# Small-head attention on one core: the preparation of the last three local batches over 24 slots in place of 16, with two preparations under way at once

## Chip, core and metric

The kernel runs on one core of a Trainium2 chip. The metric is the device time of one execution in microseconds (us), the median of several. Before the change it is 2004.02 us (three runs, 2002.38 to 2004.36).

## What is computed

The program is a chain of eight residual stages on a stream of 4 x 512 tokens of width 128, all in float32: gated linear attention, a two-layer windowed-attention block, the small-head attention of this case, the windowed block again, attention over heads, experts, full attention, experts. The stage that the change touches computes, with 16 query heads and 4 key heads of 8 elements each:

```
def global_latent_attn(x, wq, w_kv_down, w_k_up, w_v_up, wo):
    q = split_heads(x @ wq, H)
    latent = x @ w_kv_down
    k = split_heads(latent @ w_k_up, KVH)
    v = split_heads(latent @ w_v_up, KVH)
    ...
def local_gqa_attn(x, wq, wk, wv, wo):
    q = split_heads(x @ wq, H)
    k = split_heads(x @ wk, KVH)
    v = split_heads(x @ wv, KVH)
    q, k = (rope(q, BASE_L), rope(k, BASE_L))
    q, k = (qk_norm(q), qk_norm(k))
    k, v = (repeat_kv(k), repeat_kv(v))
    mask = (diff >= 0) & (diff < WIN)
    return merge_heads(sdpa(q, k, v, mask)) @ wo
```

WIN is 32. The input of the stage is a layer norm of the stream; the global attention's result is added to it, an RMS norm follows, then the local attention, and both are added to the stream.

## The kernel before

Every engine has a queue of its own that is written out by hand; between engines there are semaphores. The work of this stage is `small_heads`, one function of that name for each of TensorE (PE, L629), ScalarE (ACT, L1174), VectorE (DVE, L1701) and GpSimd (POOL, L2151).

A **batch** k is one of the 4 sequences in one of the 2 attentions: 0 to 3 are global, 4 to 7 local. A batch has four **units** U = 4k to 4k+3 (one query head of each of the four key groups), and a unit four **slots** j = 0 to 3 (key tiles of 128). In each slot PE computes transposed scores for four heads (`scores`, L678, into two PSUM pairs used in turn), ACT takes their exponential (L1210), a mask is multiplied in, by POOL for even slots (L2188) and by DVE for odd ones (L1770), and one unit later PE multiplies by the values (`values`, L691). For local batches a slot has 160 queries, for global ones up to 512. Two units later `finish` drains the sums: DVE copies them out of PSUM in slot 0 (L1777), PE transposes them back in slot 1 (L328, a helper that all transposes share), DVE divides (L1785, L1786). In the second unit of the next batch, PE transposes the heads in slot 2, ACT copies (L973, a helper), PE applies the output weights in slot 3 (L710) and DVE adds (L1794).

Beside the units of batch k runs the **preparation** of batch k+1, in 16 steps i; step i stood in slot i of the batch's 16. For a local batch:

- step 0: PE transposes the normalised stream (bank 4); DVE sums its squares (L1721 to L1725)
- step 1: ACT copies it, scaled, to `xT` (L1185)
- step 4: PE projects q into bank 4 (L652), k and v into bank 5 (L659)
- step 5: DVE copies q and k out and squares them (L1728 to L1730); step 6: sums (L1734, L1736)
- step 7: ACT takes Ln, then Exp (L1192, L1193), each with a table load ahead of it
- step 8: DVE scales q, k and v (L1742, L1743); step 9: two rotary products (L1750, L1751)
- step 10: POOL adds them (L2167); step 11: DVE makes four copies of k (L1756)
- step 12: PE transposes q and k into banks 4 and 5 (L328); step 13: ACT copies q (L973), DVE writes k four times (L1761)

Within a slot, DVE does `finish`, then the mask of an odd slot, then the preparation's step; PE does scores, `finish`, the step, values. The two lines that set this on PE are the same on the other engines but for the bound:

```
if U < 28:
    prepare(U // NR + 1, NR * (U % NR) + j)
```

The first scores of a batch wait for step 13 of its preparation on ACT and DVE (`b_qT_in`, `b_kT_in`). q and k are kept in two buffers (k % 2); the PSUM banks 4 and 5, `b_rs`, `b_ms`, `b_sq` and `xT` are single.

Of the kernel before, what the change touches and what calls it, by code (L numbers as in the profile page):

```python
# [15 lines left out]
ALU = mybir.AluOpType  # L16
# [8 lines left out]
NB = 4  # L25
S = 512
NT = S // P
# [84 lines left out]
def program(nc, x_in, w_in, c_in, r_in, out, scratch, c_at):  # L112
# [3 lines left out]
    with ExitStack() as ctx:  # L116
# [206 lines left out]
        def _(pe):  # L323
# [305 lines left out]
            def small_heads():  # L629
                unit = lambda U: (U // NR, U % NR, U < 16)  # L630

                def prepare(k, i):
                    glob = k < NB
                    if i == 0:
                        if glob:
                            pe.wait_ge(gs.ln, 2 * NB + k + 1)
                        else:
                            pe.wait_ge(s.b_add, k - NB + 1)
                        need(pe, s.b_qT_in, k)
                        transposes(4, lambda j: Y[:, NT * (k % NB) + j, :]).then_inc(s.b_xT_ps, 1)  # L640
                    elif i == 2 and glob:
                        pe.wait_ge(s.b_hT, k + 1)
                        need(pe, s.b_kT_in, k)
                        mm(ps[0:32, 5, :], W("b_down"), xT[:, :], start=True, stop=True).then_inc(s.b_lat_ps, 1)
                    elif i == 4:
                        pe.wait_ge(s.b_hT, k + 1)
                        need(pe, s.b_kT_in, k)
                        if glob:
                            pe.wait_ge(s.b_lat_in, k + 1)
                        for j in range(NT):  # L650
                            t = slice(j * P, (j + 1) * P)
                            mm(ps[:, 4, t], xT[:, t], W("b_gq" if glob else "b_lq"), start=True, stop=True)  # L652
                        for j in range(NT):
                            t = slice(j * P, (j + 1) * P)
                            o = ps[:, 5, 64 * j:64 * j + 64]
                            if glob:
                                last = mm(o, b_latT[0:32, t], W("b_up")[0:32, :], start=True, stop=True)
                            else:
                                last = mm(o, xT[:, t], W("b_lkv"), start=True, stop=True)  # L659
                        last.then_inc(s.b_kvq, 1)  # L660
                    elif i == 12:
                        pe.wait_ge(s.b_rope, k + 1)
                        pe.wait_ge(s.b_qn, k + 1)
                        transposes(4, lambda j: b_qr[:, j, 0:HB, :].rearrange("p h d -> p (h d)"))
                        pe.wait_ge(s.b_kr, k + 1)
                        transposes(5, lambda j: b_kr[:, j].rearrange("p g r d -> p (g r d)")).then_inc(s.b_tps, 1)

                def scores(U, j, gp):
                    k, r, glob = unit(U)
                    st = 8 * U + 2 * j + gp  # L670
                    if r == 0 and j == 0 and gp == 0:
                        pe.wait_ge(s.b_qT_in, k + 1)
                        pe.wait_ge(s.b_kT_in, k + 1)
                    need(pe, s.b_exp, st - 1)
                    n = small_width(glob, j)
                    for hh in range(2):
                        rows = slice(64 * gp + 32 * hh, 64 * gp + 32 * hh + 32)
                        last = mm(ps[:, 2 * (st % 2) + hh, 0:n], b_kT[rows, k % 2, r, j * P:(j + 1) * P],  # L678
                                  b_qT[rows, k % 2, j * P:j * P + n], start=True, stop=True)
                    last.then_inc(s.b_s, 1)  # L680

                def values(U, j):
                    k, r, glob = unit(U)
                    if j == 0:
                        need(pe, s.b_div, U - 1)
                        need(pe, s.b_add, k if U % 2 else 0)
                    pe.wait_ge(s.b_mask_v if j % 2 else s.b_mask_p, 2 * U + j // 2 + 1)
                    n, at = small_width(glob, j), small_at(glob, j)
                    for g in range(NG):
                        rows = slice(32 * g, 32 * g + 32)  # L690
                        last = mm(ps[rows, 6 + U % 2, j * P:j * P + n], b_vx[:, k % 2, j, g, :],  # L691
                                  b_p[:, U % 2, g, at:at + n], start=j == 0, stop=True, skip_group_check=True)
                    if j == NT - 1:
                        last.then_inc(s.b_pv, 1)

                def finish(U, j):
                    V = U - 2
                    if j == 1 and 0 <= V < 32:
                        pe.wait_ge(s.b_o_in, V + 1)
                        transposes(6 + V % 2, lambda i: b_oR[:, V % NR, i * P:(i + 1) * P]).then_inc(s.b_rT, 1)  # L700
                    k = (U - 5) // NR
                    if U % NR == 1 and 0 <= k < 2 * NB:
                        if j == 2:
                            pe.wait_ge(s.b_div, NR * k + 4)
                            transposes(7, lambda i: b_os[:, i].rearrange("p g r d -> p (g r d)"))\
                                .then_inc(s.b_oT_ps, 1)
                        elif j == 3:
                            pe.wait_ge(s.b_oT_in, k + 1)
                            for i in range(NT):
                                last = mm(ps[:, 7, i * P:(i + 1) * P], b_oT[:, i * P:(i + 1) * P],  # L710
                                          W("b_gwo" if k < NB else "b_lwo"), start=True, stop=True)
                            last.then_inc(s.b_out, 1)

                pe.wait_ge(s.b_zero, 1)
                for i in range(16):
                    prepare(0, i)
                for U in range(34):
                    for j in range(NT):
                        if U < 32:
                            scores(U, j, 0)  # L720
                            scores(U, j, 1)
                        finish(U, j)
                        if U < 28:
                            prepare(U // NR + 1, NR * (U % NR) + j)
                        if 1 <= U <= 32:
                            values(U - 1, j)

# [242 lines left out]
        def _(act):  # L970
# [203 lines left out]
            def small_heads():  # L1174
# [23 lines left out]
                for i in range(16):  # L1198
                    prepare(0, i)
                for U in range(34):  # L1200
                    k, glob = U // NR, U < 16
                    for j in range(NT):
                        if U < 32:
                            for gp in range(2):
                                st = 8 * U + 2 * j + gp
                                act.wait_ge(s.b_s, st + 1)
                                if j == 0 and gp == 0:
                                    need(act, s.b_pv, U - 1)
                                n, at, b = small_width(glob, j), small_at(glob, j), 2 * (st % 2)
                                act.activation(b_p[:, U % 2, 2 * gp:2 * gp + 2, at:at + n], ps[:, b:b + 2, 0:n],  # L1210
                                               ACT.Exp, scale=float(HD) ** -0.5).then_inc(s.b_exp, 1)
                        finish(U, j)
                        if U < 28:
                            prepare(k + 1, NR * (U % NR) + j)

            def head_attention():

# [192 lines left out]
        def _(dve):  # L1410
# [290 lines left out]
            def small_heads():  # L1701
# [99 lines left out]
                for U in range(34):  # L1801
                    for j in range(NT):
                        finish(U, j)
                        if U < 32 and j % 2:
                            mask(U, j)
                        if U < 28:
                            prepare(U // NR + 1, NR * (U % NR) + j)
                        if j == 2 and U in (2, 6):
                            fresh(U // 4 + 2)
                dve.wait_ge(s.b_add, 2 * NB)  # L1810
# [290 lines left out]
        def _(pool):  # L2101
# [49 lines left out]
            def small_heads():  # L2151
# [8 lines left out]
                        .then_inc(gs.root4, 1)  # L2160

                def prepare(k, i):
                    if i == 10 and k < 2 * NB:
                        pool.wait_ge(s.b_rt, k + 1)
                        need(pool, s.b_tps, k)
                        pairs = lambda a: a.rearrange("p j h (n b) -> p (j h n) b", b=2)
                        pool.tensor_tensor(pairs(b_qr), pairs(b_t[0]), pairs(b_t[1])[:, :, ::-1], ALU.add)\  # L2167
                            .then_inc(s.b_rope, 1)
                    elif i == 2 and k > NB:
                        z = k - NB - 1  # L2170
                        pool.wait_ge(s.b_add, z + 1)
                        x = X[:, NT * z:NT * z + NT, :]
                        pool.tensor_tensor(x, x, Y[:, NT * z:NT * z + NT, :], ALU.add).then_inc(s.b_xy, 1)

                root4()
                for i in range(16):
# [3 lines left out]
                for U in range(34):  # L2180
                    glob = U < 16
                    for j in range(NT):
                        if U < 32 and j % 2 == 0:
# [3 lines left out]
                            m = C("causal" if glob else "local", 0, n)  # L2187
                            pool.tensor_tensor(v, v, m.unsqueeze(1).broadcast_to([P, NG, n]), ALU.mult)\  # L2188
                                .then_inc(s.b_mask_p, 1)
                        if U < 32:  # L2190
                            prepare(U // NR + 1, NR * (U % NR) + j)
                        if j == 2 and U in (2, 6):
                            root4()

# [297 lines left out]
    return sum(small_width(glob, i) for i in range(j))  # L2492


def rows_at(n):

    return 0 <= n < TT
# [68 lines left out]
```

## Time and profile before

| | |
|---|---|
| runs | 2002.38, 2004.02, 2004.36 us |
| profiled execution | 2001.43 us; span of its instructions 1999.6 us |
| PE busy | 1628.7 us (81%) |
| DVE busy | 1240.1 us (62%) |
| ACT busy | 1074.5 us (54%) |
| POOL busy | 907.4 us (45%) |
| mean granted TensorE clock | 0.908 |

A time in the trace counts from the span's start. A busy time is the sum over an engine's instructions; in a timeline each row gives the start, how long it took, the engine and line, and in brackets how long the engine had stood idle before it and what released it ("issue": nothing that the profile shows). The granted clock is 1.00 at 2.4 GHz and 0.50 at 1.2 GHz. The local batches run from 953.92 us (U = 16) on.

### The profile page before, as it was taken

What the parts mean: (1) busy time and instruction counts of PE and PEld (TensorE: products, weight loads), DVE (VectorE), ACT (ScalarE), POOL (GpSimd) and SP (SyncE); (2) the same over time, 40 slices, a digit from 0 to 9 for tenths busy, and PEclk for the clock granted to TensorE, in tenths of its full rate; (3) what the DMA queues carried; (4) which work ended last, traced back from release to release, by engine and by line L of the source; (5) the groups of instructions that cost most, each with busy time, mean ns of one, the idle gap of its engine ahead of it and who ended that gap; (6) DMA issues with size and microseconds to landing.
All of it is one profiled execution on the core that took longest, in us unless ns stands there. A gap on an engine that the chain in (4) does not pass through costs nothing. (4 is left out here: it accounts for less than half of the span.)

```text
span 1999.6 us, 37978 instructions
## 1 busy us (share of the span) xinstructions
PE 1628.7 (81%) x13323; PEld 1163.0 (58%) x13323; DVE 1240.1 (62%) x3746; ACT 1074.5 (54%) x2751; POOL 907.4 (45%) x668
## 2 busy tenths in 40 slices
PE   6999996899989965888878788999976675958877
PEld 5888884566666643334544465666654453646655
DVE  4555554787777733555674687777754985736565
ACT  3555553678787732566453577777762112323432
POOL 2333333766556511223443666566622664432034
PEclk9999998999999985899876799999998896978989
DMA  4000000111111100000000011111100001110012
GB/s 200 1 1 1 1 1 9 27 27 25 30 27 25 25 6 1 1 1 1 1 1 1 19 29 31 26 26 25 25 20 1 0 0 28 26 32 1 1 43 22
DMA packets 41082, 38.64 MB, mean 19 GB/s; under 512 B 21944, under 2 KB 32192, under 8 KB 40512
## 3 DMA queue, kind: packets, MB, share of 16 engines
q1 hardware_dynamic: 35264, 32.02, 6.1%
q0 software_dynamic: 5632, 4.20, 1.7%
q8 instruction: 110, 1.80, 0.4%
q14 instruction: 76, 0.62, 0.1%
HBM read 13.14 MB, written 4.20 MB: 9 GB/s over the span
## 5 line engine op out<-in xcount | busy, mean ns | idle before, releaser
L973 ACT ACTIVATE arena<-ps 128x512 f32<-128x512 f32 (+4 forms) x670 | 356.4, 587 | 267.2 <-PE ps L328 101.9
L1210 ACT ACTIVATE arena<-ps 128x320 f32<-128x320 f32 (+4 forms) x256 | 132.6, 561 | 137.3 <-PE ps L678 134.4
L1110 ACT ACTIVATE arena<-arena,g_small 128x128 f32<-128x128 f32 x512 | 199.0, 404 | 0.5
L1606 DVE CUSTOM_DVE_ANT_0 arena<-ps,consts,g_ss 128x128 f32<-128x128 f32 x512 | 145.5, 346 | 79.8 <-PE ps L484 78.1
L2188 POOL TENSOR_TENSOR arena<-arena,consts 128x512 f32<-128x512 f32 (+1 forms) x64 | 93.7, 1464 | 195.6 <-ACT arena L1210 195.6
L328 PE MATMUL ps<-consts,arena 128*128 128x128 f32 x400 | 82.2, 344 | 108.2 <-DVE arena L1466 47.3
L2209 POOL TENSOR_TENSOR arena<-arena 128x512 f32<-128x512 f32 x64 | 82.1, 1283 | 186.5 <-DVE arena L1614 186.4
L678 PE MATMUL ps<-arena 32*128 32x160 f32 (+4 forms) x1024 | 122.3, 468 | 20.7 <-ACT arena L1210 10.2
L328 PEld LDWEIGHTS ps<-consts,arena 128*128 128x128 f32 x400 | 56.3, 173 | 139.1 <-DVE arena L1466 52.3
L1613 DVE TENSOR_TENSOR arena<-ps,tabs 128x512 f32<-128x512 f32 x128 | 87.5, 684 | 51.7 <-ACT arena L1079 45.0
L678 PEld LDWEIGHTS ps<-arena 32*128 32x128 f32 x1024 | 61.9, 213 | 88.1 <-ACT arena L1210 54.1
L1550 DVE TENSOR_REDUCE arena<-arena 128x8 f32<-128x1032 f32 x32 | 39.3, 1228 | 117.9 <-ACT arena L1030 117.9
L2219 POOL TENSOR_TENSOR g_ss<-g_ss,consts 128x8 f32<-128x8 f32 x64 | 105.5, 1648 | 7.0
L2136 POOL TENSOR_TENSOR arena<-arena,consts 128x8 f32<-128x8 f32 x32 | 52.8, 1649 | 122.2 <-PE ps L420 96.5
L585 PE MATMUL ps<-arena,weights 128*128 128x512 f32 (+1 forms) x192 | 101.6, 640 | 5.9 <-ACT arena L1139 3.9
L2259 POOL TENSOR_TENSOR arena<-arena 128x2048 f32<-128x2048 f32 x16 | 86.8, 5434 | 42.7 <-ACT arena L1232 42.7
L2222 POOL TENSOR_TENSOR g_ss<-g_ss,consts 128x8 f32<-128x8 f32 x64 | 104.8, 1638 | 0.0
L1110 ACT ACTIVATION_READ_ACCUMULATOR arena<-arena,g_small 128x1 f32 x512 | 103.8, 203 | 0.0
L2017 DVE SCALAR_TENSOR_TENSOR arena<-ps,arena 128x128 f32<-128x128 f32 x256 | 72.0, 343 | 43.8 <-PE ps L904 29.9
L2212 POOL TENSOR_TENSOR arena<-arena 128x512 f32<-128x512 f32 x64 | 81.4, 1272 | 39.0 <-issue 35.2
L742 PE MATMUL ps<-arena,consts 128*128 128x256 f32 x256 | 70.2, 435 | 34.6 <-DVE arena L1819 34.6
L691 PE MATMUL ps<-arena 128*32 128x160 f32 (+4 forms) x1024 | 87.5, 415 | 5.0 <-issue 5.0
(256 smaller groups left out, 4171.3 us busy)
## 6 DMA issues: line engine op xcount, KB each, us to landing
arena<-arena SPq DMA_DIRECT2D x112, 128.0 KB, 2.3
weights<-in_w SPq DMA_DIRECT2D x1, 5069.0 KB, 24.4
weights<-in_w SPq DMA_DIRECT2D x1, 2052.0 KB, 12.8
arena<-Y SPq DMA_DIRECT2D x64, 32.0 KB
arena<-Y SPq DMA_DIRECT2D x64, 31.8 KB
consts<-in_c SPq DMA_DIRECT2D x1, 1278.0 KB, 9.0
sorted_rows<-X SPq DMA_DIRECT2D x1, 1024.0 KB, 5.1
X<-sorted_rows SPq DMA_DIRECT2D x4, 256.0 KB, 3.7
```

The lines of the kernel that those rows point to most:

```text
L328: last = tr(ps[:, bank, j * P:(j + 1) * P], src(j), ident)
L585: mm(ps[0:m, 4 + c % 2, :], W("f_w1", at, at + m), g_hnT, start=True, stop=True)\
L678: last = mm(ps[:, 2 * (st % 2) + hh, 0:n], b_kT[rows, k % 2, r, j * P:(j + 1) * P], b_qT[rows, k % 2, j * P:j * P + n], start=True, stop=True)
L691: last = mm(ps[rows, 6 + U % 2, j * P:j * P + n], b_vx[:, k % 2, j, g, :], b_p[:, U % 2, g, at:at + n], start=j == 0, stop=True, skip_grou ...
L973: copy = lambda o, i: act.activation(o, i, ACT.Copy)
L1110: last = act.activation(g_p[:, n % 2, 4 * hf + i, :], g_sc[:, 4 * hf + i, :], ACT.Exp, scale=-1.0, bias=g_mn[:, h:h + 1], accum_out=g_rs[: ...
L1210: act.activation(b_p[:, U % 2, 2 * gp:2 * gp + 2, at:at + n], ps[:, b:b + 2, 0:n], ACT.Exp, scale=float(HD) ** -0.5).then_inc(s.b_exp, 1)
L1606: last = dve.tensor_tensor_reduce(g_sc[:, 4 * hf + i, :], ps[:, 4 + hf, i * P:(i + 1) * P], C("mask_f" if n % NT else "mask_f0"), g_ss[:, ...
L1613: tt(heads(low[0]), heads(src), table(tabs_at), ALU.mult)
L2188: pool.tensor_tensor(v, v, m.unsqueeze(1).broadcast_to([P, NG, n]), ALU.mult)\
L2219: stepped_after(pool.tensor_tensor(ss[:, 8:16], ss[:, 8:16], C("neghalf", 0, 8), ALU.pow))
L2222: pool.tensor_tensor(ss[:, 0:8], ss[:, 0:8], C("neghalf", 0, 8), ALU.pow).then_inc(gs.root, 1)
```

## The change

The preparations of batches 5, 6 and 7 (`EARLY`) are laid over 24 slots, from eight slots before the batch that they run beside. Step i stands at the offset `EARLY_SLOTS[i] - 8`: steps 0 to 3 at -8 to -5, step 4 at -1, steps 5, 6, 7 at 0, 1, 2, steps 8, 9, 10 at 4, 5, 6, step 11 at 8, step 12 at 10, step 13 at 11. Preparations 0 to 4 stay. Three waits on PE go with it. The adding of the two streams on POOL gets a function of its own and keeps its place.

```
@@ PE, prepare
-                        need(pe, s.b_qT_in, k)
+                        need(pe, s.b_ss if k in EARLY else s.b_qT_in, k)
                         transposes(4, lambda j: Y[:, NT * (k % NB) + j, :]).then_inc(s.b_xT_ps, 1)
...
                     elif i == 4:
                         pe.wait_ge(s.b_hT, k + 1)
+                        need(pe, s.b_qT_in, k)
                         need(pe, s.b_kT_in, k)
...
                     elif i == 12:
                         pe.wait_ge(s.b_rope, k + 1)
                         pe.wait_ge(s.b_qn, k + 1)
+                        if k + 1 in EARLY:
+                            pe.wait_ge(s.b_hT, k + 2)
@@ PE, ACT, DVE alike
-                        if U < 28:
-                            prepare(U // NR + 1, NR * (U % NR) + j)
+                        for k, i in prepared_at(NR * U + j):
+                            prepare(k, i)
@@ POOL
-                    if i == 10 and k < 2 * NB:
+                    if i == 10:
...
-                    elif i == 2 and k > NB:
-                        z = k - NB - 1
-                        pool.wait_ge(s.b_add, z + 1)
-                        x = X[:, NT * z:NT * z + NT, :]
-                        pool.tensor_tensor(x, x, Y[:, NT * z:NT * z + NT, :], ALU.add).then_inc(s.b_xy, 1)
+                def add_streams(z):
+                    pool.wait_ge(s.b_add, z + 1)
+                    x = X[:, NT * z:NT * z + NT, :]
+                    pool.tensor_tensor(x, x, Y[:, NT * z:NT * z + NT, :], ALU.add).then_inc(s.b_xy, 1)
...
-                        if U < 32:
-                            prepare(U // NR + 1, NR * (U % NR) + j)
+                        for k, i in prepared_at(NR * U + j):
+                            prepare(k, i)
+                        if j == 2 and U in (16, 20, 24, 28):
+                            add_streams((U - 16) // NR)
@@ new
+EARLY = (5, 6, 7)
+EARLY_SLOTS = (0, 1, 2, 3, 7, 8, 9, 10, 12, 13, 14, 16, 18, 19, 20, 21)
+
+def prepared_at(slot):
+
+    return [(k, i) for k in range(1, 2 * NB) for i in range(16)
+            if slot == 16 * (k - 1) + (EARLY_SLOTS[i] - 8 if k in EARLY else i)]
```

In the changed kernel the lines of DVE and ACT stand 3 further down (L1761 is L1764, L1777 is L1780, L1770 is L1773, L1756 is L1759, L1721 is L1724, L1210 is L1213, L1192 is L1195).

**DVE, third unit of a local batch (U = 18, with the preparation of batch 5), up to the copy of the fourth.** Before:

```order
L1777 COPY arena<-ps 128x512
L1742 TENSOR_TENSOR arena<-arena,b_rs 128x640
L1743 TENSOR_TENSOR arena<-ps,b_rs 128x16x8
L1785 RECIPROCAL b_ri<-ps 128x16
L1786 TENSOR_TENSOR arena<-ps,b_ri 128x16x8
L1770 TENSOR_TENSOR arena<-arena,consts 128x4x160
L1750 TENSOR_TENSOR arena<-arena,consts 128x640
L1751 TENSOR_TENSOR arena<-arena,consts 128x640
L1770 TENSOR_TENSOR arena<-arena,consts 128x4x128
L1756 COPY arena<-arena 128x16x8 x4
L1777 COPY arena<-ps 128x512
```

and of the change, from the same L1777 (now L1780) to that of the unit after:

```order
L1780 COPY arena<-ps 128x512
L1759 COPY arena<-arena 128x16x8 x4
L1724 TENSOR_TENSOR arena<-Y 128x4x128
L1726 TENSOR_REDUCE b_rs<-arena 128x4
L1727 TENSOR_SCALAR b_rs<-b_rs 128x4
L1728 TENSOR_SCALAR b_ms<-b_rs 128x4
L1788 RECIPROCAL b_ri<-ps 128x16
L1789 TENSOR_TENSOR arena<-ps,b_ri 128x16x8
L1773 TENSOR_TENSOR arena<-arena,consts 128x4x160
L1773 TENSOR_TENSOR arena<-arena,consts 128x4x128
L1764 TENSOR_SCALAR arena<-ps,consts 128x512 x4
L1780 COPY arena<-ps 128x512
```

Steps 8 and 9 have left the third unit, and steps 11 and 13 of this preparation and step 0 of the next have come in; step 13 (L1764) now stands between the unit's last mask and the copy of the next unit.

**ACT, the exponentials around step 7 (preparation of batch 7).** Before, after the exponentials of a second unit's last slot (128 queries):

```order
L1210 ACTIVATE arena<-ps 128x2x160 x6
L973 ACTIVATE arena<-ps 128x512
L1210 ACTIVATE arena<-ps 128x2x128 x2
L1192 ACT_TABLE_LOAD
L1192 ACTIVATE b_rs<-b_rs 128x84
L1193 ACT_TABLE_LOAD
L1193 ACTIVATE b_rs<-b_rs 128x84
L1210 ACTIVATE arena<-ps 128x2x160 x6
```

and of the change, before the exponentials of the first unit's last slot:

```order
L1213 ACTIVATE arena<-ps 128x2x160 x6
L1195 ACT_TABLE_LOAD
L1195 ACTIVATE b_rs<-b_rs 128x84
L1196 ACT_TABLE_LOAD
L1196 ACTIVATE b_rs<-b_rs 128x84
L1213 ACTIVATE arena<-ps 128x2x128 x2
L1213 ACTIVATE arena<-ps 128x2x160 x6
```

The two table loads are as many as before; they have moved from between the second and third unit into the first.

## Rows read from the trace of the kernel before

**Rows 1.** The page: its first line.

```profile
span 1999.6 us, 37978 instructions
```

**Rows 2.** Stretches: length, busy time (instructions) by engine, granted clock, DMA share, GB/s.

```profile
953.92:990.52 36.60, 30.48 (x312) 17.53 (x313) 24.64 (x43) 16.48 (x39) 16.27 (x10) 0.77 0.01 1
990.52:1024.65 34.13, 27.88 (x313) 17.14 (x313) 24.84 (x43) 16.48 (x39) 16.61 (x10) 0.80 0.01 1
...
1060.00:1076.90 16.90, 16.90 (x141) 10.04 (x140) 5.29 (x11) 5.95 (x16) 7.80 (x5) 0.50 0.00 1
1077.00:1086.00 9.00, 8.66 (x118) 5.23 (x120) 4.78 (x9) 5.30 (x14) 4.75 (x4) 1.00 0.01 3
```

**Rows 3.** Timeline of PE, third and fourth unit beside preparation 6, and next start.

```profile
1005.63 0.48 PE L691 MATMUL ps<-arena 128*32 128x160 f32 x8 [1.57 <-issue]
1007.20 0.87 PE L678 MATMUL ps<-arena 32*128 32x160 f32 x8 [1.09 <-ACT arena L1210]
...
1014.87 1.11 PE L328 MATMUL ps<-consts,arena 128*128 128x128 f32 x4 [1.75 <-POOL arena L2167]
1016.86 1.11 PE L328 MATMUL ps<-consts,arena 128*128 128x128 f32 x4 [0.87 <-DVE arena L1756]
...
1024.65 0.55 PE L678 MATMUL ps<-arena 32*128 32x160 f32 x8 [0.85 <-DVE arena L1761]
```

**Rows 4.** Timeline of PE: start of unit 16, and step 4 of preparation 6.

```profile
953.92 0.70 PE L678 MATMUL ps<-arena 32*128 32x160 f32 x8 [0.98 <-issue]
...
996.33 1.16 PE L652 MATMUL ps<-weights,xT 128*128 128x128 f32 x8
997.33 1.00 PE L659 MATMUL ps<-weights,xT 128*128 128x64 f32 x8
```

**Rows 5.** Timeline of PE: starts of units 25, 28, 29, 30, and output weights.

```profile
1029.79 0.74 PE L678 MATMUL ps<-arena 32*128 32x160 f32 x8
...
1058.75 0.55 PE L678 MATMUL ps<-arena 32*128 32x160 f32 x8 [0.85 <-DVE arena L1761]
...
1065.79 0.92 PE L678 MATMUL ps<-arena 32*128 32x160 f32 x8
...
1073.46 2.08 PE L710 MATMUL ps<-weights,arena 128*128 128x128 f32 x8
...
1076.05 0.92 PE L678 MATMUL ps<-arena 32*128 32x160 f32 x8
```

**Rows 6.** Timeline of DVE: steps 5 to 6, 11, 13, a mask, L1777, step 0.

```profile
1001.08 0.68 DVE L1728 COPY arena<-ps 128x512 f32<-128x512 f32 x1
...
1004.69 0.24 DVE L1736 SCALAR_TENSOR_TENSOR b_rs<-b_rs,b_ms 128x80 f32<-128x80 f32 x1
...
1014.85 1.95 DVE L1756 COPY arena<-arena 128x128 f32<-128x128 f32 x4 [1.43 <-POOL arena L2167]
...
1021.83 2.72 DVE L1761 TENSOR_SCALAR arena<-ps,consts 128x512 f32<-128x512 f32 x4
1024.47 0.68 DVE L1770 TENSOR_TENSOR arena<-arena,consts 128x512 f32<-128x512 f32 x1
1025.07 0.68 DVE L1777 COPY arena<-ps 128x512 f32<-128x512 f32 x1
1025.67 0.68 DVE L1721 TENSOR_TENSOR arena<-Y 128x512 f32<-128x512 f32 x1
...
1028.02 0.26 DVE L1785 RECIPROCAL b_ri<-ps 128x16 f32<-128x16 f32 x1
...
1028.52 0.81 DVE L1770 TENSOR_TENSOR arena<-arena,consts 128x640 f32<-128x640 f32 x1
```

**Rows 7.** Timeline of ACT: step 7 of preparation 6, and the exponentials behind it.

```profile
1002.84 1.28 ACT L1192 ACT_TABLE_LOAD   x1
1004.97 0.27 ACT L1192 ACTIVATE b_rs<-b_rs 128x84 f32<-128x84 f32 x1 [0.84 <-DVE b_rs L1736]
...
1006.73 0.75 ACT L1210 ACTIVATE arena<-ps 128x320 f32<-128x320 f32 x2
```

More of the change, by code:

```diff
@@ L1200, in small_heads @@
                 for U in range(34):
-                    k, glob = U // NR, U < 16
+                    glob = U < 16
                     for j in range(NT):
@@ L1212, in small_heads @@
                         finish(U, j)
-                        if U < 28:
-                            prepare(k + 1, NR * (U % NR) + j)
+                        for k, i in prepared_at(NR * U + j):
+                            prepare(k, i)
             def head_attention():
@@ L1805, in small_heads @@
                             mask(U, j)
-                        if U < 28:
-                            prepare(U // NR + 1, NR * (U % NR) + j)
+                        for k, i in prepared_at(NR * U + j):
+                            prepare(k, i)
                         if j == 2 and U in (2, 6):
@@ L2189, in small_heads @@
                                 .then_inc(s.b_mask_p, 1)
-                        if U < 32:
-                            prepare(U // NR + 1, NR * (U % NR) + j)
+                        for k, i in prepared_at(NR * U + j):
+                            prepare(k, i)
+                        if j == 2 and U in (16, 20, 24, 28):
+                            add_streams((U - 16) // NR)
                         if j == 2 and U in (2, 6):
```

## The prediction, made before the changed kernel had run

> **What bounds the kernel now.** The execution's span is 1999.6 us [rows 1]; I first cut out the stage that changes by batches. The local batches beside which a preparation runs take 36.60 us and 34.13 us [rows 2], the third 34.10 us (from 1024.65 [rows 3] to 1058.75 [rows 5]); the last, with no preparation beside it, is some 27 us to its last values. In the 34.13 us no engine is full: PE is busy 27.9, DVE 24.8, ACT 16.5, POOL 16.6 [rows 2]. So no engine's sum is the bound but the order in which they wait for each other, and I went on to PE's timeline.
>
> There PE stands idle five times per batch [rows 3]: 1.57 us and 1.09 us as the third unit starts, 1.75 us and 0.87 us at step 12, 0.85 us before the next batch's first scores. The first is put down to nothing, but `values` waits there for `b_add`, and DVE comes to L1794 only behind steps 5 and 6. The second is ACT's, behind the table loads of step 7 [rows 7]. The third and fourth are step 12 waiting for steps 10 and 11, the fifth is step 13 (L1761, 2.65 us from its start to the next mask [rows 6]). In all 6.13 us. The granted clock is the other half: 0.80 over the batch. A unit at full clock takes 5.14 us with step 0 in it (1024.65 [rows 3] to 1029.79 [rows 5]), one at half clock 7.04 us without a step (1058.75 to 1065.79), and 10.26 us with the output weights in it (1065.79 to 1076.05, L710 alone 2.08) [rows 5].
>
> **The change part by part.** No instruction is added or taken away; I walk a batch of the changed kernel unit by unit, t from each unit's start, from these rows.
>
> *Waits that go.* Step 5 and 6 are no longer ahead of L1794 (1.57 us). Between steps 10, 11 and 12 there are now two slots each: POOL's add is done a unit before L1756 wants it, and L1756 before PE wants it (1.75 and 0.87 us). Step 13 ends a unit before the next batch (0.85 us). What is late next is below. POOL's queue gets step 10 ahead of another mask, nothing else; the adding of the streams stays; SP has nothing in this stage.
>
> *First unit.* DVE does L1777 (0.6), steps 5 and 6 (3.85, from 1001.08 to the end of L1736 at 1004.93), between them a division (0.5) and a mask (0.6 to 0.75) [rows 6]: it ends at 5.75 us, or up to 6.45 us where POOL's masks slow it. ACT has then loaded its table and waits, as it does now for 0.84 us; from Ln to the next exponentials is 1.76 us (1004.97 to 1006.73) [rows 7], from there to PE's next scores 0.47 (1007.20 [rows 3]). So the second unit starts at 8.0 to 8.7 us; I take 8.4, nearer the crowded end since POOL masks twice there. PE has work for about 4.5 us of it (5.14 less step 0): it idles nearly 4 us at a stretch. The table loads cost more than the 2.66 us of today, since DVE's steps 5 and 6 start only with the unit.
>
> *Second unit.* After 1.57 and 1.09 us of idling PE fell to half clock today (the L678 behind it takes 0.87 in place of 0.55 [rows 3]); after 4 us it will too. The unit is then unit 29 again: 10.26 us at half clock throughout, some 9.6 with the first slots still at full; I take 10.0. Steps 8, 9 on DVE and 10 on POOL lie beside it.
>
> *Third unit.* In unit 29 the clock came back behind L710 (1.00 from 1077 us on [rows 2]). So full clock: 5.14 with step 0, and step 12, 8 transposes, which took 1.1 for four at half clock [rows 3] and so some 1.3 for eight at full: 6.7 with its queueing. DVE does L1777, L1756 (up to 1.95 beside a POOL mask), step 0 and a division (2.85, from 1025.67 to 1028.52), a mask [rows 6]: some 6.2 us, beside PE. The added wait of step 12 for `b_hT` is for ACT's copy one slot before, done by then: nothing; uncovered it would be one copy of 512 columns, some 0.6 as DVE's [rows 6]. Behind it on PE stand values and all scores. Step 0's wait on `b_ss` was met nearly a unit earlier.
>
> *Fourth unit.* Here is the new wait. DVE's queue reads: mask of the third unit's last slot, step 13, then L1777, and PE's transposes in slot 1 wait for that copy. The mask can start at 0.2 us, when the exponentials are done; 0.6 + 2.65 + 0.6 [rows 6] puts the copy's end at 4.1 us. PE is there after one slot and one pair of scores, at 1.4. It idles 2.7 us. Behind it are two and a half slots and step 4: 3.2 (5.14 less step 0 and the 1.4) and 2.0 [rows 4], so 5.3 at full clock; at half 4.7 and 4.1, so 8.8. PE fell to half clock after 0.85 us of idling before unit 28 [rows 5], so it will here; step 4's dense matmuls should bring it back. I take 7.6, the unit 11.7.
>
> A batch: 8.4 + 10.0 + 6.7 + 11.7 = 36.8 us, for the batches of units 16 to 19 and 20 to 23. Beside units 24 to 27 there are no steps 0 and 4: third unit 6.2 (step 12 waits for L1756), fourth 4.1 and between 3.2 and 4.7, I take 4.5: 8.4 + 10.0 + 6.2 + 8.6 = 33.2.
>
> *Ahead of it.* Step 0 of preparation 5 moves into global unit 14, where it lies in a wait that ACT sets; step 4 into the last slot of unit 15. There it waits for `b_kT_in`, as unit 16's scores do for 0.98 us [rows 4], and so that wait is not made longer but by 0.35, and its own 2.0 us come on top: 2.4 us. It would be 0 only if PE had that long to wait there, which it has not.
>
> **The sum.** 2.4 + 2 x 36.8 + 33.2 = 109.2 us against 36.60 + 34.13 + 34.10 = 104.8: 4.4 us longer. The last batch keeps its 27 us: it was at half clock from just after its start [rows 5] and will be. The profiled execution ran 2001.43 us, so 2005.8 for it; the median of the runs stands 2.6 higher, so 2008.4. A measurement of this kernel can tell about 0.2%, 4 us, from no change.
>
> Bounds: with the fourth unit's rest at full clock it is 2.3 x 2 + 1.3 less (minus 1.5 in all), and with the first unit 0.4 and the second 0.4 shorter, three times, minus 3.9; with rest, first and second unit at their upper ends, plus 8.7.
>
> **A rule against the trace.** From 1060 to 1076.9 us PE was busy for 16.90 of 16.90 us and stayed at 0.50 all the time [rows 2]. The Trainium skill ("TensorE: Matmul & The Clock Gate", Part 1, What's actually happening) holds that "the default state is throttled, and activity releases the throttle", by how busy PE has been. By that rule alone a gapless second unit would soon be back at full clock; this trace does not agree for a stretch of 32-row scores and values, and only with L710 did the clock rise. The rival that follows is the first below.
>
> **The rivals.**
> *The clock comes back early in the second unit.* The unit then takes 5.14 less step 0's 0.6 plus 0.6 for the head transposes and 1.1 for L710 at half its 2.08, wait by wait 6.9 in all with its queueing. DVE becomes the bound after it: L1794 and mask 1.2, L1777 0.6, L1756 1.95, step 0 and division 2.85, two masks 1.35, step 13 2.65, L1777 0.6 make 11.2 from the third unit's start to PE's transposes in the fourth. A batch is 8.4 + 6.9 + 11.2 + 5.3 = 31.8, the third 28.8 (mask and step 13 behind its exponentials): 2.4 + 63.6 + 28.8 = 94.8, 10 us shorter than before; with the fourth unit's rest at half clock 4 shorter. I put 7 shorter, 1997. For it: the second unit has two sets of dense transposes and L710. Against: unit 29 had the same and came up only at its end. It decides from a rise before the middle of the unit.
> *The clock holds in the fourth unit* although PE idles 2.7 us: 1.5 us shorter than before, 2002.5. For it: at units 20 and 24 the 0.85 us cost no clock, dense transposes being near (unit 24 to 25 is full clock [rows 3, 5]). Against: the gap is three times as long.
> *The clock never rises* in the third unit: 7.04 + 1.1 + 2.2 = 10.4 for it, the fourth 1.3 of waiting, 7.04 and 4.1 = 12.4, batch 42: 15 to 20 us slower, 2021. For it: today the batches' 0.80 means 40% of 34 us, 14 us, at half clock [rows 2], well past one unit; against: L710.
> *The copy is not waited for*, because PE comes later than I reckon. Then the fourth unit saves 2.7 us; that needs a third unit over 9 us, which is no gain either, so it has no number of its own.
>
> **How the numbers follow.** My forecast, half clock in most of the fourth unit: 0.54, of which 0.34 is over 4 us slower and 0.20 within. The clock holds: 0.18 (0.15 within, 0.03 faster). It comes back early: 0.20, all faster. It never rises: 0.08, slower. Faster 0.23, same 0.35, slower 0.42. The range: 1998 takes in the lower bound and a third of the early clock, 2015 the upper bound; outside lie some 0.12 below and 0.07 above.
>
> **What would show it.** In the changed profile: no idle time of L328 released by POOL's add or by the copies of step 11; no wait at `values` for L1794; in each first unit a PE gap near 4 us up to the exponentials of its last slot; in each fourth unit one near 2.7 us before the transposes, released by the copy L1780; half clock through the second unit and into the fourth. Wrong if the fourth unit's gap is below 1 us, or if the second unit takes 7 us.

## The result and the profile after

| | before | changed |
|---|---|---|
| median (18 runs each, taken together) | 1999.56 us | 2007.71 us |
| lowest to highest | 1996.84 to 2007.59 | 2004.62 to 2013.47 |
| profiled execution: span | 1999.6 us [rows 1] | 2008.7 us |
| mean granted clock | 0.908 | 0.903 |

The changed kernel takes 1.004 times as long, 95% interval 1.003 to 1.0049: 8 us slower. The first three runs of before had a median of 2004.02 us; over 18 it is 1999.56, so the forecast of 2008.4 was 4.4 us of loss on a base that was 4.5 us high. That it lies so near 2007.71 is luck: a loss that was too small and a base that was too high.

The page of the changed kernel:

```profile
span 2008.7 us, 37984 instructions
PE 1637.3 (82%) x13323; PEld 1170.4 (58%) x13323; DVE 1237.7 (62%) x3746; ACT 1073.2 (53%) x2751; POOL 906.1 (45%) x668
```

The matmuls are the same in number (13323), as are those of DVE, ACT and POOL; PE's busy time is 8.6 us longer at a mean granted clock of 0.903 in place of 0.908. The stage cut by batches, as in [rows 2] (length, busy by engine, granted clock, DMA, GB/s); the rows begin at the first scores of units 16, 20, 24 and 28, the last is the tail at full clock:

```profile
957.47:997.37 39.90, 31.77 (x317) 19.02 (x313) 25.86 (x42) 16.38 (x39) 16.22 (x10) 0.76 0.00 1
997.37:1036.30 38.93, 34.11 (x317) 21.40 (x313) 23.03 (x42) 16.37 (x39) 16.22 (x10) 0.63 0.01 1
1036.30:1069.48 33.18, 28.68 (x296) 16.64 (x293) 19.75 (x38) 15.80 (x38) 16.18 (x10) 0.65 0.00 1
1069.48:1085.50 16.02, 16.02 (x152) 9.25 (x148) 5.60 (x11) 6.51 (x17) 8.04 (x6) 0.57 0.00 1
1085.50:1096.00 10.50, 10.16 (x148) 6.18 (x144) 6.06 (x12) 6.02 (x16) 5.64 (x4) 1.00 0.01 2
```

Unit 16 starts 3.55 us later (957.47, 953.92 in [rows 4]); then 39.90 against 36.60, 38.93 against 34.13, 33.18 against 34.10 us; and the last batch up to unit 31 gives back 1.6. That is +3.6 (unit 15 grew by 4.0 and 0.5 came off ahead of unit 14), +3.3, +4.8, -0.9, -1.6: 9.1 us, all of the spans' difference. In the second batch the clock is 0.63 where it was 0.80.

PE's timeline of that second batch, where [rows 3] had five gaps:

```profile
997.37 0.92 PE L681 MATMUL ps<-arena 32*128 32x160 f32 x8
...
1006.92 1.18 PE L681 MATMUL ps<-arena 32*128 32x160 f32 x8 [2.06 <-ACT arena L1213]
...
1014.63 2.08 PE L713 MATMUL ps<-weights,arena 128*128 128x128 f32 x8
...
1017.22 0.92 PE L681 MATMUL ps<-arena 32*128 32x160 f32 x8
...
1023.71 0.82 PE L681 MATMUL ps<-arena 32*128 32x160 f32 x8
...
1028.29 0.71 PE L328 MATMUL ps<-consts,arena 128*128 128x128 f32 x4 [2.61 <-DVE arena L1780]
...
1032.11 2.08 PE L653 MATMUL ps<-weights,xT 128*128 128x128 f32 x8
1033.98 1.81 PE L660 MATMUL ps<-weights,xT 128*128 128x64 f32 x8
1036.30 0.92 PE L681 MATMUL ps<-arena 32*128 32x160 f32 x8
```

The rows of L681 are the starts of units 20 to 24: 9.55, 10.30, 6.49 and 12.59 us. All five old gaps are gone; two new ones stand where the forecast put them, before the second unit's first scores (3.04 us in the first batch, 2.06 in the other two) and before the fourth unit's transposes. Step 4 runs at half clock (2.08 and 1.81 us; 1.16 and 1.00 in [rows 4]). DVE's timeline shows why the second gap is there; it answers to [rows 6]:

```profile
1022.79 2.20 DVE L1773 TENSOR_TENSOR arena<-arena,consts 128x640 f32<-128x640 f32 x2
1024.92 2.71 DVE L1764 TENSOR_SCALAR arena<-ps,consts 128x512 f32<-128x512 f32 x4
1027.55 0.68 DVE L1780 COPY arena<-ps 128x512 f32<-128x512 f32 x1
```

Two masks, step 13, then the copy that PE wants, 4.5 us after the fourth unit's start at 1023.71. In unit 19 the same gap is 4.85 us, in unit 27 2.27 us. What makes unit 19's so long is the last mask ahead of step 13, on DVE, which starts beside a mask of POOL:

```profile
983.62 2.03 DVE L1773 TENSOR_TENSOR arena<-arena,consts 128x512 f32<-128x512 f32 x1
```

```profile
983.57 1.53 POOL L2191 TENSOR_TENSOR arena<-arena,consts 128x640 f32<-128x640 f32 x1 [1.45 <-ACT arena L1213]
```

It takes 2.03 us there and 0.69 in unit 27, where it stands alone.

### The profile page after: what moved, and what is told of

Its sections match the earlier page's. It is cut to its first block and busy times, and to the rows that moved or that the text cites. A ratio compares the mean times of both kernels' runs of the same rounds, so it can differ in the third digit from the quotient of the medians.

```text
span 2008.7 us, 37984 instructions
## 1 busy us (share of the span) xinstructions
PE 1637.3 (82%) x13323; PEld 1170.4 (58%) x13323; DVE 1237.7 (62%) x3746; ACT 1073.2 (53%) x2751; POOL 906.1 (45%) x668
## 5 line engine op out<-in xcount | busy, mean ns | idle before, releaser
L1213 ACT ACTIVATE arena<-ps 128x320 f32<-128x320 f32 (+4 forms) x256 | 132.1, 561 | 148.5 <-PE ps L681 145.6
L681 PE MATMUL ps<-arena 32*128 32x160 f32 (+4 forms) x1024 | 125.9, 484 | 20.9 <-ACT arena L1213 13.8
L681 PEld LDWEIGHTS ps<-arena 32*128 32x128 f32 x1024 | 64.3, 223 | 90.5 <-ACT arena L1213 59.8
L907 PEld LDWEIGHTS ps<-weights,arena 128*128 128x128 f32 x512 | 69.4, 198 | 38.7 <-issue 36.8
```

Source lines behind the costliest of these rows:

```text
L907: last = mm(ps[:, 6 + q % 2, j * P:(j + 1) * P], e_h[:, q % 2, j * P:(j + 1) * P], W("e_w2", 128 * e, 128 * e + 128), start=True, stop=True)
```

## The experiments

Lengths of units come from PE's timeline in each run's profile, as above. Ratios are to the kernel before, run on the same chip.

### Step 13 two slots later

```
-                    elif i == 13:
+                    elif i == (15 if k in EARLY else 13):
                         dve.wait_ge(s.b_tps, k + 1)
```

> The changed kernel with one move: DVE's part of step 13 (four writes of k) stands two slots later, in slot 1 of the fourth unit behind its mask, in place of slot 3 of the third. Theory A (the copy of the fourth unit stands in the queue behind step 13, and PE waits for the copy): the gaps of 4.85, 2.61 and 2.27 us before the fourth units' transposes shrink to under 1 us, units 19, 23 and 27 (15.25, 12.59, 9.06 us) take about 8, 8 and 6.5, and the kernel is 12 to 14 us faster than the changed one, so 4 to 6 us faster than the one before. Theory B (DVE is simply full in the third unit, whatever the order): the gap stays over 2 us, or comes back as a wait of step 4 for the keys, and the time stays within 3 us of the changed kernel's, 5 to 8 us above the one before.

Measured: 2001.28 us, ratio 1.0008 (0.9993 to 1.0023); about 6 us faster than the changed kernel, level with before, and half of theory A's 12 to 14. The gaps before the fourth units' transposes are 2.22 and 0.66 us, and none in the third batch, from 4.85, 2.61 and 2.27; units 19, 23, 27 take 12.92, 10.74 and 6.64 us. So the order of the queue alone is worth 6 us. Theory B holds for the rest: step 4 on PE, and at the end the scores of unit 28, now wait for the keys.

```profile
1023.83 0.66 PE L328 MATMUL ps<-consts,arena 128*128 128x128 f32 x4 [0.66 <-DVE arena L1780]
...
1028.62 1.20 PE L653 MATMUL ps<-weights,xT 128*128 128x128 f32 x8 [1.90 <-DVE arena L1764]
```

### PE's gap filled with matmuls

```
                         if 1 <= U <= 32:
                             values(U - 1, j)
+                        if U in (16, 20, 24) and j == 3:
+                            pe.wait_ge(s.b_div, U - 1)
+                            for _ in range(12):
+                                tr(ps[:, 6, 384:512], ident, ident)
```

> The kernel of step13_late, with 12 transposes of a constant matrix added on PE behind the values of the last slot in units 16, 20 and 24, where PE waits for the table loads (their results are never read). Theory A (the second unit is slow because PE idles ahead of it and falls to half clock): with the gap filled the second units run at full clock, 7 us in place of 9 to 10, and the kernel is 4 to 8 us faster than step13_late. Theory B (the second unit takes what its waits on ACT and DVE make it, the clock hardly counts): its length stays within 1 us and the kernel within 2 us of step13_late.

Measured: 2000.77 us, ratio 1.0005 (0.9993 to 1.0017); not to be told from step13_late, so theory A's 4 to 8 us did not come. But the profile shows both halves of the rival that I had priced. Units 20 and 21 (first scores of the second unit at 1003.55, of the third at 1009.78), in PE's timeline and, below it, as stretches with the clock in the last but two columns:

```profile
1001.11 2.51 PE L733 MATMUL ps<-consts 128*128 128x128 f32 x12
1003.55 0.55 PE L681 MATMUL ps<-arena 32*128 32x160 f32 x8
...
1013.26 1.02 PE L328 MATMUL ps<-consts,arena 128*128 128x128 f32 x4 [1.17 <-DVE arena L1784]
```

```profile
1003.55:1009.78 6.23, 6.12 (x81) 3.97 (x80) 5.89 (x9) 3.44 (x9) 3.83 (x2) 1.00 0.01 3
1009.78:1018.65 8.87, 7.39 (x84) 4.55 (x80) 8.70 (x15) 3.31 (x9) 5.04 (x3) 0.81 0.00 0
```

With the gap filled the second unit ran at 1.00 and took 6.23 us, against 10.31 in step13_late (7.40 against 8.76, 6.23 against 10.31 in the other two batches). The third unit took 8.87 against 6.38, with DVE busy 8.70 of the 8.87 us. Over the three batches 9.5 us were won in the second units and 6.7 lost in the third: clock gained ahead of a full DVE is given back at DVE. The rest went in units 28 to 30, 22.50 us in place of 19.92, at a granted clock of 0.62 in place of 0.74.

### The table loads left out, in both kernels

```
-                        after(act.activation(b_rs[:, :], b_rs[:, :], ACT.Ln))
-                        act.activation(b_rs[:, :], b_rs[:, :], ACT.Exp, scale=-0.5).then_inc(s.b_rn, 1)
+                        fn = (ACT.Ln, ACT.Exp, -0.5) if k <= NB else (ACT.Copy, ACT.Copy, 0.003)
+                        after(act.activation(b_rs[:, :], b_rs[:, :], fn[0]))
+                        act.activation(b_rs[:, :], b_rs[:, :], fn[1], scale=fn[2]).then_inc(s.b_rn, 1)
```

> The changed kernel, where ACT applies two copies with a scale in place of Ln and Exp in step 7 of the preparations 5 to 7: left out are the reciprocal roots, so q, k and v have other sizes, and with them the two table loads of each. Theory A (the changed kernel's first unit ends with the table loads): units 16, 20, 24 (9.98, 9.55, 9.55 us) lose 2 to 3 us each, 7 to 9 us in all and a few more where the clock then stays up; 8 to 12 us faster than the changed kernel. Theory B (DVE's steps 5 and 6 set the end of the first unit): ACT then waits for them, and less than 3 us is gained.

> The kernel before with the same left out (the reciprocal roots of preparations 5 to 7, and the two table loads of each). Theory A (there PE's wait for b_add behind steps 5 and 6 on DVE covers more than half of the loads): 1.1 us less at each start of the third unit, 3 to 5 us in all with the clock. Theory B (the loads cost the same in both): 8 to 12 us.

Measured, changed kernel: 2001.55 us, ratio 1.0009 (0.9994 to 1.0024), some 6 us faster than with the loads. Units 16, 20, 24 take 8.67, 7.44 and 7.42 us, 1.3 to 2.1 less each, 5.6 in all: less than the 7 to 9 of theory A and more than theory B's 3. (The batch in which DVE's last mask meets POOL's changed too: the gap of the fourth unit is 2.61 us in the first batch and 4.93 in the second.) Kernel before: 1999.85 us, ratio 1.0 (0.9989 to 1.0012), nothing. There the third unit's gap of 1.09 us went and the fourth unit's grew from 1.75 [rows 3] to 4.26:

```profile
1013.06 1.12 PE L328 MATMUL ps<-consts,arena 128*128 128x128 f32 x4 [4.26 <-POOL arena L2168]
```

Step 12 waits there for POOL's add, and that for DVE's steps 8 and 9. On DVE, the stretch ahead of it:

```profile
1004.75 1.85 DVE L1743 TENSOR_TENSOR arena<-arena,b_rs 128x640 f32<-128x640 f32 x1
...
1007.33 2.21 DVE L1771 TENSOR_TENSOR arena<-arena,consts 128x640 f32<-128x640 f32 x1
```

Each of the two stands beside one of POOL's masks (1004.37 and 1007.31, 1.55 us each) and takes 1.0 and 1.4 us longer than the 0.82 of such an operation alone. Counted from the first scores of unit 20, step 8 starts 16.13 us in, where it started 16.34 us in with the loads, for DVE's own queue comes to it no sooner; step 11 stands at 24.41 in place of 24.33. So the loads were no bound of the kernel before: they were covered by DVE's queue and the chain DVE, POOL, DVE behind it. Whether something would have been gained had the two operations not met POOL's masks, this run does not show.

### DVE's part of step 13 on ACT, in both kernels

```
                         copy(b_qT[:, k % 2], ps[:, 4, :]).then_inc(s.b_qT_in, 1)
+                    if k > NB and i >= 13:
+                        for r in ((0,), (1, 2), (3,))[i - 13]:
+                            ins = act.activation(b_kT[:, k % 2, r, :], ps[:, 5, :], ACT.Copy, scale=C("rows", r, r + 1))
+                        if i == 15:
+                            ins.then_inc(s.b_kT_in, 1)
...
-                    elif i == 13:
+                    elif i == 13 and k <= NB:
                         dve.wait_ge(s.b_tps, k + 1)
```

> The changed kernel with DVE's part of step 13 (2.65 us a batch) given to ACT for the preparations 5 to 7: four scaled copies out of PSUM, one, two and one in the slots of steps 13, 14 and 15. Theory A (in the third unit DVE's queue is the bound, and filling PE's gap gained nothing for that reason): the fourth units' gaps before the transposes go under 0.5 us without the wait of step 4 that moving step 13 brought; 9 to 14 us faster than the changed kernel, 1 to 6 us faster than the one before. Theory B (the length of a batch is set by the chain through POOL and ACT): ACT's four copies delay the exponentials by as much, and it is no faster than step13_late, 2 us above the one before.

> The kernel before with the same edit. Theory A: only the 0.85 us before each batch's first scores goes, and some of PE's waits for the copies of step 12 stay (1.75 and 0.87 us): 2 to 3 us faster in all. Theory B (any work taken from DVE shortens the batch by as much): 6 to 8 us faster.

Measured, on the changed kernel: 1985.4 us, ratio 0.9943 (0.9925 to 0.9962): 0.6% faster than before (11 us by the ratio, 14 by the medians) and some 20 us faster than the changed kernel, well over theory A's 9 to 14. Its batches:

```profile
956.45:989.08 32.63, 28.66 (x317) 16.84 (x313) 22.22 (x38) 18.63 (x43) 16.22 (x10) 0.85 0.01 1
989.08:1020.40 31.32, 26.36 (x317) 16.67 (x313) 22.74 (x38) 18.63 (x43) 16.34 (x10) 0.89 0.01 2
1020.40:1049.51 29.11, 24.14 (x296) 14.81 (x292) 19.11 (x33) 17.73 (x42) 15.70 (x10) 0.88 0.01 1
```

and the fourth unit of the second, PE first, then ACT's last three writes between the exponentials:

```profile
1015.29 0.66 PE L328 MATMUL ps<-consts,arena 128*128 128x128 f32 x4 [0.38 <-DVE arena L1785]
...
1018.11 1.16 PE L653 MATMUL ps<-weights,xT 128*128 128x128 f32 x8
```

```profile
1013.53 0.79 ACT L1218 ACTIVATE arena<-ps 128x320 f32<-128x320 f32 x2
1014.16 1.31 ACT L1202 ACTIVATE arena<-ps,consts 128x512 f32<-128x512 f32 x2
1015.30 0.82 ACT L1218 ACTIVATE arena<-ps 128x320 f32<-128x320 f32 x2
1015.94 0.77 ACT L1202 ACTIVATE arena<-ps,consts 128x512 f32<-128x512 f32 x1
```

The gap is 0.38 us, step 4 waits for nothing and runs at full clock; the fourth units take 7.94, 8.03 and 5.81 us, from 15.25, 12.59 and 9.06. More than DVE's 2.65 us per batch was won since the gap was also what lowered the clock: 0.89 in the second batch, 0.63 before the edit. It shows behind the preparations too. Units 28 to 30, which have no preparation beside them and were not edited, as stretches with the columns of [rows 2], first in the kernel before, then here:

```profile
1058.75:1081.46 22.71, 22.43 (x216) 13.28 (x216) 8.23 (x16) 9.48 (x25) 10.09 (x7) 0.62 0.01 1
```

```profile
1049.51:1066.09 16.58, 16.19 (x221) 10.11 (x217) 9.90 (x16) 9.47 (x26) 10.98 (x8) 1.00 0.01 2
```

The same work takes 6.1 us less at 1.00 than at 0.62 (21.09 us at 0.67 in the changed kernel), and so these three units hold more than a third of the 15.7 us by which the two spans differ.

On the kernel before the same edit lost: 2006.54 us, ratio 1.0035 (1.0022 to 1.0047), where both theories had a gain. The last write stands one slot ahead of the next batch's first scores, and ACT makes it only after the exponentials of that slot's neighbours:

```profile
1024.88 0.92 PE L678 MATMUL ps<-arena 32*128 32x160 f32 x8 [0.94 <-ACT arena L1199]
1025.72 1.12 PE L328 MATMUL ps<-consts,Y 128*128 128x128 f32 x4
```

The wait is 0.94 us (1.48 in the first batch) for 0.85, and units 20 and 24 run partly at half clock, 6.59 and 7.14 us for 5.14; the third units after them take 9.67 and 9.68 for 8.70 and 8.68. In unit 20 the clock fell behind the wait. In unit 24 it had not come back ahead of it: it stood at 0.50 from unit 23's first scores through the wait, where in the kernel before it rose in unit 23's last slots (0.90 from 1021.9 us on). Why it does not rise there here, the runs do not settle.

### Preparation 5 back in its place

```
-EARLY = (5, 6, 7)
+EARLY = (6, 7)
```

> The changed kernel with preparation 5 back in its 16 slots; 6 and 7 stay spread. Theory A (my sum: ahead of unit 16 the change costs 2.4 us, the trace shows 4.0, and unit 16 is 2.4 us longer): units 15 and 16 are back at 18.3 from 24.7 us, and the kernel is 5 to 7 us faster than the changed one, 1 to 3 us slower than before. Theory B (those 6 us come back as waits in units 17 to 19, since preparation 5 has then to be made beside them): within 2 us of the changed kernel.

Measured: 2011.01 us, ratio 1.0064 (1.0047 to 1.008), 3 us slower than the changed kernel by the medians and 5 by the ratios, whose intervals just touch; not the gain of theory A. Units 15 and 16 are back at 10.69 and 7.63 us, as theory A had it, but unit 19 takes 19.67 us:

```profile
982.16 1.12 PE L328 MATMUL ps<-consts,arena 128*128 128x128 f32 x4 [4.95 <-POOL arena L2170]
```

Step 0 of preparation 6 now stands on DVE right behind step 8 of preparation 5 (973.22 to 977.3 us, L1724 to L1728), ahead of step 9, and POOL and PE wait for step 9. So theory B had the place of the loss right: the 6 us of units 15 and 16 are no pure loss of the change, and here they come back beside units 16 to 19 with more on top.

### An early start without the spreading

```
-            if slot == 16 * (k - 1) + (EARLY_SLOTS[i] - 8 if k in EARLY else i)]
+            if slot == 16 * (k - 1) + (i - {5: 2, 6: 4, 7: 4}.get(k, 0))]
```

with step 0's wait on `b_qT_in` as before and without the wait of step 12 on `b_hT`.

> The kernel before with preparation 5 started two slots earlier and 6 and 7 four, each in 16 consecutive slots: an early start without the spreading and without two in banks 4 and 5 at once. Theory A (PE's waits come from steps of one preparation in neighbouring slots): L328's 1.75 and 0.87 us stay, the 1.57 us at values goes since L1794 no longer stands behind steps 5 and 6, and so do the 0.85 us: 2 to 5 us faster than before. Theory B (an early start fills the first unit as in the changed kernel, with the table loads' gap at PE in full): 3 to 8 us slower.

Measured: median 1996.98 us, ratio 1.0013 (0.9993 to 1.0033): no difference that can be told. But its twelve times lie in two groups, seven from 1994.41 to 1997.1 us at a granted clock of 0.913 to 0.917 and five from 2006.83 to 2007.63 at 0.906; the one fits theory A's 2 to 5 us, the other theory B's loss, and what parts them no trace shows, for the profile is of the first group. In it theory A's 1.57 and 0.85 us are gone, and so, against it, are the 1.75 and 0.87, but for 0.50 us in the second batch; theory B's gap of the table loads is there in full:

```profile
1006.84 1.23 PE L679 MATMUL ps<-arena 32*128 32x160 f32 x8 [3.82 <-ACT arena L1211]
```

New are waits of 1.86 to 2.56 us for the copy L1778 in each of units 16 to 19. That batch takes 40.94 us (36.60 before), the next two 33.80 and 32.42 (34.13 and 34.10), and units 28 to 30 16.57 at a clock of 1.00 (22.71 at 0.62).

### Two more on the faster version

`k_on_act_filled` adds the 12 transposes of filled_gap; `k_on_act_four` lets ACT write the keys of preparation 4 too (`k >= NB`, and `k < NB` on DVE).

> The kernel of k_on_act_after with the 12 constant transposes of filled_gap in the gaps of units 16, 20 and 24. In filled_gap the second units became 1.4 to 4.1 us shorter and the third 1.4 to 2.8 us longer, because DVE was the bound. Theory A: with DVE relieved of step 13 the gain of the second units is kept: units 17, 21, 25 (8.76, 8.51, 8.22 us) take 6.5 to 7.4, the third units stay below 7, and it is 3 to 5 us faster than k_on_act_after. Theory B (DVE is the bound there even so, or the transposes delay PE as much as the clock gives back): within 1.5 us of it.

> The kernel of k_on_act_after with ACT writing the keys for preparation 4 as well, which runs beside the wide global units and ends in unit 15. Theory A: the 1.38 us for which step 4 of preparation 5 waits on DVE's writes in unit 15, and part of the half clock after it, go: 1 to 3 us faster than k_on_act_after. Theory B: ACT has exponentials of up to 512 queries there and its four copies delay them; 0 to 3 us slower.

Measured: 1986.58 us, ratio 0.993 (0.9916 to 0.9944), and 1991.71 us, ratio 0.9958 (0.9939 to 0.9976). The first cannot be told from k_on_act_after; the medians differ by 1.2 us, as in theory B. But theory A's premise was not met: with the first unit at full clock the transposes take 1.53 us in place of 2.51, a gap is left, and the clock fell all the same (0.64 over unit 21, which took 9.46 us; 0.57 and 0.56 over units 17 and 25):

```profile
994.62 1.53 PE L733 MATMUL ps<-consts 128*128 128x128 f32 x12
998.30 0.81 PE L681 MATMUL ps<-arena 32*128 32x160 f32 x8 [2.15 <-ACT arena L1222]
```

So what a steady clock would bring once DVE is relieved stays open; a filling matched to the gap was not tried. The second is slower in its median, though its times spread from 1981 to 2000 us and the intervals overlap: step 4 in unit 15 waits 1.88 us for ACT's last write in place of 1.38 for DVE's, theory B's side.

## The prediction, point by point

*Right.* The direction, for the reason that was given. The range 1998 to 2015 held 2007.71. The five old waits went, and the two new ones came where they were forecast. In the fourth unit DVE's order mask, step 13, copy makes PE wait for L1780 (forecast 2.7 us; 4.85, 2.61, 2.27), and step13_late and k_on_act_after show that it is this order and this 2.65 us. The clock falls with it and step 4 runs at half (forecast fourth unit 11.7 and 8.6; 15.25, 12.59, 9.06). The last spread batch was forecast at 33.2 and took 33.18, but by luck: its four units were off by +1.2, -1.2, -0.4 and +0.5. The second unit was forecast at 10.0 and took 8.74, 10.30 and 8.79; the third at 6.7, 6.7 and 6.2 against 5.93, 6.49 and 5.78. The rival of an early clock was worth what filled_gap shows: 6.2 us for the second unit (6.9 in its price), and DVE as the bound behind it.

*Too small.* The sum, 4.4 us, against 8 by the medians and 9.1 by the spans: 1.2 are missing ahead of unit 16, 3.1 in the first batch and 2.1 in the second, none in the third, and the last batch was 1.6 too long. Term by term:

- "Ahead of it", 2.4 us: unit 15 grew by 4.0. Step 4 waits 1.38 us for L1764 and then runs at half clock (1.87 and 1.81 us, forecast 2.0 for both). I had priced its matmuls at full clock right behind a wait, while pricing the same pair at half clock in the fourth units.
- "First unit", 8.4 us: 9.98, 9.55 and 9.55. I had PE at full clock and DVE's steps 5 and 6 as the end, and of step 4 I had written that its dense matmuls should bring the clock back. They did not: from 993.17 us, where step 4 starts in unit 19, to 1004.86 PE was busy all the 11.69 us at 0.50, and so again behind unit 23. So in the second and third batch the clock was still low from the fourth unit's gap: some 1.1 us of work per slot became 1.5, the exponentials of slot 2 ended 6.1 us after the unit's start, when DVE was done too, and ACT went from the load to Ln with no idle time. PE's gap was 2.06 us, not near 4. In the first batch the values of unit 15, up to 512 wide, kept PE as long, and L1739 at the end of step 6 took 1.61 us beside POOL's mask in place of 0.24; the gap is 3.04. ACT's timeline of the second batch, which answers to [rows 7]:

```profile
1003.44 1.28 ACT L1195 ACT_TABLE_LOAD   x1
1004.73 0.27 ACT L1195 ACTIVATE b_rs<-b_rs 128x84 f32<-128x84 f32 x1
...
1006.50 0.64 ACT L1213 ACTIVATE arena<-ps 128x256 f32<-128x256 f32 x2
```

- "Fourth unit" of units 16 to 19, 11.7 us: 15.25. DVE came to the third unit's last mask 1.5 us into the unit (forecast 0.2), and that mask stood beside POOL's (L1773 at 983.62 took 2.03 us, forecast 0.6), so the copy ended 6.8 us after the unit's start, not 4.1. Behind the gap PE ran at half clock to the end.
- "Second unit", 10.0 us, with the clock back only behind L710: in units 17 and 25 it was back behind the second set of four transposes, ahead of the output weights (L713 took 1.16 us there and 2.08 in unit 21), and they took 8.74 and 8.79 us. These 1.2 us each hide part of the loss in the first units.
- "The last batch keeps its 27 us": it gave back 1.6 up to unit 31. (The 27 us reach to its last scores; its last values end at 1090.2 us, 31 us after its start.)

The first two have one root: a unit was priced from full clock, and the low clock that it has from the gap or the unit ahead was left out. The third has another: what DVE's operations take beside POOL's masks.

## What to carry to other kernels

Waits between engines can be moved off one engine and the kernel still be no faster: ask of each step in its new slot which instruction stands behind it in that queue and who waits for that. Here the spreading was sound and one step of 2.65 us on the engine that the others wait for cost more than all it saved: some 20 us in all (k_on_act_after), 6 of them by its place in front of a 0.6 us copy (step13_late). Given to the engine with room, in pieces between its own work, it left a version 0.6% faster than the start. Look also at the stretch behind the one you change: over a third of that gain lies in units that nothing was done to, and is clock. And try such a relief together with the schedule that needs it: on the kernel before it lost 7 us.

## What was not expected

An operation of DVE that reads two tensors in SBUF takes far longer while POOL's mask runs: 1.85 and 2.21 us in place of 0.82 (no_tables_before), 2.03 in place of 0.6 to 0.7 (changed kernel, unit 18's last mask). The kernel before has it too (step 5's product L1730 took 1.81 us beside a mask), so it could have been read ahead of the change. Even the scaling of 4 columns did, which reads one tensor and took 0.17 us elsewhere (k_on_act_after, DVE, then the POOL mask beside it):

```profile
1011.12 1.36 DVE L1732 TENSOR_SCALAR b_rs<-b_rs 128x4 f32<-128x4 f32 x1
```

```profile
1010.91 1.54 POOL L2196 TENSOR_TENSOR arena<-arena,consts 128x640 f32<-128x640 f32 x1 [1.64 <-ACT arena L1218]
```

DVE's ends at 1012.48, when POOL's does at 1012.45: it waited rather than ran slowly. The Trainium skill ("SBUF — State Buffer", Who interferes with whom) says that only the port pair that DVE and GpSimd share contends, as an exclusive lock, that a DVE operation with two SBUF inputs falls under it, that a tensor_scalar can in its two-port modes, and that a tensor reduction on this chip never does. The traces agree with the lock and with both kinds of operation in the numbers above. They agree on the reduction too: in the kernel before, L1723 at 992.25 us kept its 0.69 us under a mask of POOL (991.94, 1.69 us), and the scaling of 4 columns right behind it ended with that mask (0.68 us in place of 0.17). So moving a step changes its price, by what POOL does there.

The clock fell after a gap of 2.15 us that followed 1.53 us of gapless 128-row transposes (k_on_act_filled, unit 21), and after gaps of 1.69 and 2.14 us behind the same transposes (units 17 and 25). But in filled_gap, in the first batch, it held at 1.00 through unit 17 behind the same 1.53 us and a gap of 1.57. So work ahead of a gap did not surely hold it; what decided, these four gaps do not show. With 2.51 us of transposes and no gap behind (filled_gap, unit 20) it stood at 1.00 through the whole second unit, while in the kernel before 16.9 gapless us of the same scores, values and sets of transposes stood at 0.50 [rows 2].
